# Two attention layers on one core: the output product of block 2 behind the next pair's scores, with a new order of the steps

## The reference, cut to what matters

```python
# block 1
z  = mha(x, x, Wq1, Wk1, Wv1, causal=True);         x1 = layernorm(x + z)
z  = mha(x1, context, Wq2, Wk2, Wv2, causal=False); x2 = layernorm(x1 + z)
h  = layernorm(x2 + (relu(x2 @ fc1.T + b1) @ fc2.T + b2))
# block 2: q from h, k and v from the context, bias added twice
scores  = (h @ wq + bq) / 8 @ k.T + 2 * bias
weights = softmax(scores)                # 16 heads of 64 x 64
out = layernorm((weights @ v) @ wo + bo + h)
```

## Time and profile before

| | |
|---|---|
| median of 3 runs | 397.06 us (396.39 to 400.57) |
| the profiled execution | 397.58 us, its span 395.4 us |
| PE busy | 345.0 us, 87% of the span |
| DVE, ACT, POOL busy | 293.4, 232.7, 235.7 us |
| granted TensorE clock, mean | 0.956 of full speed |

### The profile page before, as it was taken

How to read it: one execution, slowest core, us unless ns; L and a number is a source line. 1 busy time by engine, 2 the same in 40 slices (tenths; PEclk the granted TensorE clock), 3 DMA queues, 4 the chain that set the end, 5 groups by cost and what they waited for, 6 DMA issues and landing times.

```text
span 395.4 us, 13051 instructions
## 1 busy us (share of the span) xinstructions
PE 345.0 (87%) x5296; PEld 240.2 (61%) x5296; DVE 293.4 (74%) x833; ACT 232.7 (59%) x561; POOL 235.7 (60%) x372
## 2 busy tenths in 40 slices
PE   2868979899999999999999999999999978776644
PEld 1434535658686868585858586868675747364533
DVE  3554793897989898979797989797979675735141
ACT  1314625485858686767677676768685837363421
POOL 0135161658485858585858585858686665665361
PEclk9968889999999999999999999999999999999955
DMA  5991000010001010102020202020202020101000
GB/s 163 325 342 48 0 2 2 2 55 3 2 2 61 5 61 3 61 2 61 5 61 4 61 2 61 5 61 2 61 5 61 2 61 2 61 2 61 8 8 7
DMA packets 13178, 17.86 MB, mean 45 GB/s; under 512 B 1600, under 2 KB 10176, under 8 KB 13120
## 3 DMA queue, kind: packets, MB, share of 16 engines
q1 hardware_dynamic: 13120, 17.04, 13.9%
HBM read 15.99 MB, written 1.05 MB: 43 GB/s over the span
## 4 chain that ended last, share of the span: by engine, by line
PE 73%; POOL 8%; DVE 7%; ACT 6%; issue 4%; DMA 1%; SPq 1%; POOLq 0%; ACTq 0%; DVEq 0%
PE C_E L455 8%; PE C_E L537 7%; PE C_E L488 6%; PE C_E L469 6%; PE C_E L514 4%; PE C_E L528 4%; PE A_E L365 4%; PE C_E L503 3%; PE B_E L365 3%; PE A_E L398 2%; PE B_E L398 2%; PE B_E L384 2%; POOL B_kblk L888 2%; PE B_X L384 2%; PE A_X L384 2%
## 5 line engine op out<-in xcount | busy, mean ns | idle before, releaser
L568 ACT ACTIVATE A_S<-A_S 128x512 f32<-128x512 f32 x32 | 20.2, 631 | 65.8 <-DVE A_S L766 65.8
L888 POOL TENSOR_TENSOR A_kblk<-A_qk,cst 128x1024 f32<-128x1024 f32 x16 | 30.4, 1898 | 41.1 <-DVE A_qk L734 39.8
L896 POOL TENSOR_TENSOR L_ve<-L_mv,cst 128x1 f32<-128x1 f32 x64 | 12.3, 192 | 61.4 <-DVE L_mv L799 61.3
L929 POOL TENSOR_TENSOR Sc<-Sc,mxc 128x512 f32<-128x512 f32 x32 | 33.4, 1044 | 22.2 <-DVE mxc L846 22.2
L907 POOL TENSOR_TENSOR L_xg<-L_xh,vec_sb 128x128 f32<-128x128 f32 x64 | 29.4, 459 | 17.9 <-DVE L_xh L808 17.9
L898 POOL TENSOR_TENSOR L_rstd<-L_ve,cst 128x1 f32<-128x1 f32 x64 | 35.2, 551 | 5.0
L537 PEld LDWEIGHTS C_E<-wo_sb,C_zT 128*128 128x128 f32 x256 | 31.4, 200 | 11.1 <-ACT C_zT L633 11.1
L537 PE MATMUL C_E<-wo_sb,C_zT 128*128 128x128 f32 x256 | 34.6, 291 | 3.5 <-ACT C_zT L633 3.5
L455 PE MATMUL C_E<-cTs,wk_sb 128*128 128x512 f32 x64 | 36.0, 645 | 0.3 <-DVE Sc L837 0.3
L938 POOL TENSOR_TENSOR Pc<-Pc,rdc 128x512 f32<-128x512 f32 x32 | 33.0, 1045 | 4.8 <-DVE rdc L856 4.8
L646 ACT ACTIVATE qT<-C_E,bq 128x128 f32<-128x128 f32 x128 | 34.8, 384 | 0.7 <-PE C_E L488 0.7
(11 more groups left out here) (148 smaller groups left out, 954.5 us busy)
## 6 DMA issues: line engine op xcount, KB each, us to landing
f<-in_fs SPq DMA_DIRECT2D x16, 512.0 KB, 4.1
out<-osb SPq DMA_DIRECT2D x16, 64.0 KB, 2.0
xTs<-in_xT SPq DMA_DIRECT2D x1, 768.0 KB, 8.7
xs<-in_x SPq DMA_DIRECT2D x1, 768.0 KB, 10.7
cs<-in_ctxn SPq DMA_DIRECT2D x1, 768.0 KB, 12.4
cTs<-in_ctxT SPq DMA_DIRECT2D x1, 768.0 KB, 9.8
vec_sb<-in_vecs SPq DMA_DIRECT2D x1, 640.0 KB, 6.9
wk_sb<-in_wk SPq DMA_DIRECT2D x1, 512.0 KB, 4.3
```

Source lines behind the costliest of these rows:

```text
L888: tt(a.kblk[:], a.qk[:, 1].unsqueeze(1).to_broadcast([P, 8, P]), at["rmask"].unsqueeze(2).to_broadcast([P, 8, P]), ALU.mult).then_inc(a.s_ ...
L929: tt(v, v, mxc[:, 8 * g:8 * g + 8].unsqueeze(2).to_broadcast([P, 8, S]), ALU.subtract).then_inc(C.s_sub, 1)
```

## The change

Two waits are taken from one place and put at others, and the order table is new.

- C.e (pair n) waits for both halves of the copy of z of the pair before instead of for its C.y.
- C.o (pair n) now stands on PE behind C.e of pair n + 1, and so waits for the first C.fadd of pair n + 1, which has read bank 0. Its sum and norm (C.y, C.st, C.xh, C.rstd, C.gb) move into the softmax of pair n + 1.
- The next writers of bank 0 (the first half of C.k, and for the last pairs of C.v or C.pt) wait for C.y.
- All other steps keep their instructions; their numbers in `TURN` change, and `SHIFT` gets small values per pair. Its rows D and E are read by nothing.

```diff
@@ C.k, first half, from the fifth pair on
                         pe.wait_ge(C.s_s, 2 * (n - FIRST) + 1 + g)
+                        if g == 0 and n > FIRST:
+                            pe.wait_ge(L4.s_y, n - FIRST)
@@ C.v, last three pairs
                         pe.wait_ge(C.s_s, 2 * n - 1 + b)
+                        if b == 0:
+                            pe.wait_ge(L4.s_y, n - 1)
@@ C.e
                 if n:
-                    pe.wait_ge(L4.s_y, n)
+                    pe.wait_ge(C.s_zts, 2 * n)
@@ C.pt
+                    if g == 0 and n == PAIRS - 1:
+                        pe.wait_ge(L4.s_y, n)
@@ C.o
                     pe.wait_ge(C.s_zts, 2 * n + 1 + r)
+                    if r == 0 and n + 1 < PAIRS:
+                        pe.wait_ge(C.s_s, 2 * n + 3)
@@ TURN
-C.zts_1=-0.1903111 C.o_0=-0.1675396 C.o_1=-0.1404375 C.st=0.1958135 C.xh=0.2584186 C.rstd=0.3205016
+C.zt=-0.4571533 C.zts_1=-0.4562809 C.o_0=-0.3010685 C.o_1=-0.2879722 C.rstd=0.1108049 C.gb=0.2344158
```

More of the change, by code:

```diff
@@ L977 @@
-C.gb=0.7617832
+C.loadf=-25.6352937 C.store=-25.4628038 A.m0=-8.0374611 A.q0=-6.8567084 A.nz=-6.6590799 A.qkv=-6.6228260
+A.cut=-6.5168082 A.qk=-6.5087926 A.kblk=-6.5055931 A.v=-6.5030362 A.e0=-6.3865391 A.cnt=-6.2280970
+A.max_0=-5.9342174 A.max_1=-5.9204896 A.sub_0=-5.8838610 A.sub_1=-5.8761223 A.e=-5.5070108 A.zn=-5.4553665
+A.rstd=-5.4427902 A.exp_0=-5.3845715 A.pt_0=-5.3719892 A.pt_1=-5.3610652 A.y=-5.3337244 A.exp_1=-5.3069099
+A.st=-5.3029932 A.pv_0=-5.2040256 A.pts_0=-5.1979065 A.pv_1=-5.1808642 A.pts_1=-5.1762682 A.xh=-5.1622335
@@ new lines @@
+A.zts=-5.0931185 C.k_0=-5.0762621 A.z=-5.0747224 C.ks_0=-4.9846167 C.ks_1=-4.9362786 C.k_1=-4.9110372
+A.gb=-4.9016980 B.am=-4.6185636 B.q0=-4.2642148 B.nz=-4.1028434 B.cm=-4.0908534 B.kblk=-4.0617173
+B.tr=-4.0154863 B.cut=-4.0098549 B.v=-3.9853294 B.xts=-3.9596655 B.max_0=-3.7651046 B.qkv=-3.7645178
+B.max_1=-3.7622724 B.qk=-3.6893486 B.sub_0=-3.6709640 B.sub_1=-3.6648840 B.e0=-3.6110392 B.cnt=-3.5810994
+B.e=-3.4312926 B.pt_0=-3.2663392 B.zn=-3.2572493 B.pt_1=-3.2551888 B.y=-3.2505708 B.pv_0=-3.1677104
@@ new lines @@
+B.rstd=-3.1599189 B.st=-3.1349838 B.exp_0=-3.1326207 B.exp_1=-3.1236401 B.pts_0=-3.1185392 B.pv_1=-3.1143926
+B.pts_1=-3.1131994 B.zts=-2.9826717 B.xh=-2.9722977 B.gb=-2.9500080 B.z=-2.7147438 B.3rstd=-2.6870842
+B.3gb=-2.6717123 B.y3=-2.6253260 B.3st=-2.6185610 B.3xh=-2.5417281 B.f1=-2.4152429 B.f2=-2.3462528
+C.obias=-2.3035625 B.f3=-2.2963961 B.f1s=-2.2470617 B.f2s=-2.1762645 C.vs_0=-1.8751882 C.v_0=-1.8562476
+C.v_1=-1.7815922 C.vs_1=-1.7610384 C.bvo=-1.7448149 C.x3t=-1.7215002 C.x3ts=-1.7191682 C.sub_0=-1.7078654
@@ new lines @@
+C.q_0=-1.6816221 C.q_1=-1.6816201 C.fadd_0=-1.6788385 C.max_0=-1.6447005 C.fadd_1=-1.5908809 C.qs_0=-1.5783861
+C.qs_1=-1.5776975 C.sub_1=-1.5477630 C.max_1=-1.5135141 C.e=-1.3936754 C.den_0=-1.3364072 C.den_1=-1.2447641
+C.nrm_0=-1.2110440 C.nrm_1=-1.1912117 C.x3c=-1.1782872 C.exp_0=-0.8829641 C.exp_1=-0.7327149 C.y=-0.6224477
+C.pts_0=-0.5592887 C.pt_0=-0.5450190 C.pt_1=-0.5347100 C.pts_1=-0.5284668 C.zts_0=-0.4759593 C.st=-0.4631637
+C.zt=-0.4571533 C.zts_1=-0.4562809 C.o_0=-0.3010685 C.o_1=-0.2879722 C.rstd=0.1108049 C.gb=0.2344158
@@ L978 @@
+C.xh=0.3285207
 """
 SHIFT = """
-A 0 0 0 0 0 0 0 0 0 0 0 0 0 0 0 0
-B 0 0 0 0 0 0 0 0 0 0 0 0 0 0 0 0
-C 0 0 0 0 0 0 0 0 0 0 0 0 0 0 0 0
+A -0.0213503 0.0028653 -0.0010209 -0.0150977 -0.0135021 0.0406371 0.0058127 -0.0008013 -0.0040836 0.0159683 0.0143593 0.0130246 0.0085384 0.001457 0.0193181 0.018252
+B -0.0086425 0.004721 -0.0084863 0.0113124 0.0063089 -0.0009638 0.009332 -0.0005828 0.0128892 -0.0044063 0.0067991 -0.0097093 -0.0088663 -0.0054933 0.0085909 0.0013406
+C -0.0079447 -0.0022421 -0.005616 -0.0167521 -0.0176205 -0.011139 -0.0052958 -0.0017445 -0.0095533 -0.0047654 -0.0070014 -0.004989 -0.0090162 -0.0082186 -0.0002872 -0.0327468
@@ L983 @@
+D -16.66969 -13.67604 -13.2421 -12.00916 -4.085415 -4.694634 -2.385743 0.8940692 2.734035 6.373563 6.299987 6.51613 8.416475 8.1427 11.31833 15.27481
+E -10.31015 -11.09027 -10.10759 -6.36055 -5.250412 -5.006341 0.2840603 2.312384 4.743302 5.012065 8.032633 11.0436 15.61534 14.70947 15.16696 15.12085
 """
```

## The result

The changed kernel took 408.75 us (median of 4 runs, 407.09 to 410.65) against 397.19 us (396.39 to 400.57) for the kernel before on the same chip: a ratio of 1.0276, 95% interval 1.0202 to 1.0350. That is +11.6 us; predicted were 404.9 us, between 394.5 and 411. The profiled execution has a span of 406.5 us (408.69 us), at a mean granted clock of 0.961.

What follows compares the result with a forecast made beforehand. PE's own work and short in-order waits bound the middle, chain C's latency the end. Start +1.0, middle +6.6 and end -0.3 gave +7.3 on 397.6: 404.9 us, 8-in-10 range 394.5 to 411, the forecast's own 401 to 409.

Steps and rivals of the forecast that it cites:

- The removed wait: Scores' wait for C.y: hidden by A's qkv in the middle, gain nothing; at the end scores come 2.0 us sooner.
- The middle, +6.6: Nine periods between the scores of pairs 1 and 10: 0.73 us more each than 20.06, together +6.6 us.
- five items: Pieces of one middle period, second C.k to the next: 4.52, 3.52, 2.18, 2.35 and 8.28, together 20.85 us.
- The start, +1.0: Pipeline fill up to the scores of pair 1: +1.0 us, between -1 and +4; chain A's first step 3.1 to 4.0 late.
- idle time of PE can absorb some: In the start: PE stands 20.8 us, nearly all before 98.74, which can take up part of the delay.
- The end, -0.3: From the scores of pair 10 on: +0.7, four periods -2.1, last pair +1.1; sum -0.3 us, between -3.5 and +2.
- the sentence on the clock: Last stretch: if the clock stayed up, z product and C.o would give back 2.5 us; counted as 0.
- in-order wait for C.y: Last pair's softmax: DVE has C.y ahead of the second maximum; second transposes 8.95 us after scores instead of 7.86, +1.1.
- 1 (PE at its bare work): Rival: faster, middle periods at PE's bare 19.2 to 19.7 us, 390 us in all; chance 0.14.
- 2: Rival: within one per cent, period stays 20.0 to 20.3, 397 to 399 us; chance 0.23, shared with an undersized forecast.
- 3 (DVE or POOL in the loop): Rival: clearly slower, each may cost 0.5 us more per period, 21.5 us, 411; chance 0.10 shared with the fourth rival.
- 4 (the change frees nothing): Rival: copy of z no earlier than C.y, so no 2 us in four periods, 407 us; beyond 409, 0.10 with the third.

Runs made afterwards that it cites:

- e8_late1: The kernel before, with the new place of C.o and C.y and the new wait of C.e only behind pair 14: 395.33 us, ratio 0.9968.
- e3_nocover: The kernel before, with the transpose of h (C.x3t) put directly before q on PE: 407.25 us, ratio 1.0153.
- e9_cover: The changed kernel, with the transpose of h (C.x3t) ahead of B's qkv, waiting only for the first half of V's copy: 403.07 us, ratio 1.0133.
- e2_tail: The changed kernel, with C.y(14) and its variance on DVE between the two halves of the last pair's denominator: 407.06 us, ratio 1.0237.
- e4_move: The kernel before's order table with the new waits and only C.o, C.y and C.k's first half moved as those need: 431.09 us, ratio 1.0773.
- e5_order: The new order table with the old waits and the old place of C.o and C.y: 434.71 us, ratio 1.0853.

## Why the prediction was right, point by point

- **The removed wait is worth nothing in the middle, 2.0 us at the end**: right. Scores follow the z product by 2.35 us in the middle, by 2.40 at the end (382.60 - 380.20) against 4.35, and e8_late1 earned 1.96 with it alone.
- **The middle, +6.6**: measured +5.5. All five items came out within 0.1, the sum by 0.19 too large against a period of 20.66 (the prediction took 20.8), since the period is a little shorter in other pairs than in the one read. Its cause, q without cover behind the transpose of h, was shown twice: e3_nocover made it in the old order (+0.57), e9_cover took it away in the new one (-0.40). The rest of +0.61 is 0.2 us that e9_cover left (20.26 against 20.06); that wasn't tested alone. The 0.3 for short products in the rival's bare work of 19.2 us stands in no row, and the forecast doesn't use it.
- **The start, +1.0**: mis-sized, +3.4 measured. The first step of chain A came 2.6 us late (10.18 against 7.62; predicted 3.1 to 4.0), and "idle time of PE can absorb some" was right: without falls of the clock, 3.0 us at e0 became 1.2 at the scores of pair 1. What the sum left out is the clock in the fill, which it put at nothing without a word: in the changed kernel's execution it fell twice between 30 and 50 us, and e2_tail with the same fill and no such fall had the scores of pair 1 at 101.17 instead of 102.11, though it was 1.4 us behind at A's second scores (29.25 against 27.84). So two falls cost some 2.3 us. The bound (+4) held. What the other terms named there are worth (C.o out, B's scores in, and the later scores of A) stays open, since the kernel before lost clock in its fill as well (0.66 to 0.85 between 20 and 60 us).
- **The end, -0.3**: the sign failed, +2.3 measured. The periods themselves were right: at a clock of 1.00, 20.21, 18.28, 17.56 and 16.45 (predicted 20.2, 18.4, 17.9 and 16.5, by a working that isn't shown). What failed was the sentence on the clock, which saw only a possible gain and counted 0. The clock took 21.60 - 20.21 = 1.4 us in the period behind pair 11. In the last pair it took C.o of pair 14 to 3.55 us, with which the in-order wait for C.y, predicted at +1.1, became +2.6 (10.44 against 7.86). "If the clock stayed up" didn't come true: the last C.o took 3.79 us as before.
- **Compensation**: of the total, 11.1 us of span against 7.3 predicted, the start gave 2.4 more, the end 2.6 more, and the middle 1.1 less. The falls of the clock in the changed kernel's execution, some 2.3 us in the fill, 1.4 behind pair 11 and 1.5 at C.o of pair 14, are together more than the 3.8 us that were missing; what the kernel before had lost in its own fill isn't known. The same kernel, measured again, took 412.63 us, so that the first set of runs fell inside the range is in part luck.
- **Rivals**: 1 (PE at its bare work) is refuted by the middle. 2 fails by the same rows. 3 (DVE or POOL in the loop) is refuted for the changed kernel by e9_cover; it is what happened in e4_move and e5_order. 4 (the change frees nothing) is refuted at the end by e8_late1. Its 407 us takes back the net 2.1 us of four periods, not four times 2.0.

## What to carry to other kernels

When a step moves, ask first what it had been covering: on an engine that works in order, 1.9 us of output product had covered another chain's POOL latency, by the waits of e4_move, and moving them alone cost 2.0 us a period. For each short step that goes out through another engine and back, write down the round trip (0.68 us here, PE to ACT to PE) and count the work that stands between in the new order; that adding gave the period to 0.2 us from a trace of the old kernel. Where it wasn't done step by step, for e4_move and e5_order, the expected periods were 1.7 and 1.3 us too short. And compare the starts of two kernels only between executions whose clock did the same. A latency that only the last pairs feel is best removed in the last pairs alone.
